# Two stacked GRU layers and a mixture of experts on one core: a PSUM bank for each gate, and PE work by gate

## What is computed

```python
def _gru_layer(x, Wih, Whh, bih, bhh):
    xg = jnp.einsum('bti,gi->tbg', x, Wih) + bih
    def step(h, xt):
        hg = h @ Whh.T + bhh
        xr, xz, xn = jnp.split(xt, 3, axis=-1)
        hr, hz, hn = jnp.split(hg, 3, axis=-1)
        r = jax.nn.sigmoid(xr + hr)
        z = jax.nn.sigmoid(xz + hz)
        n = jnp.tanh(xn + r * hn)
        h_new = (1.0 - z) * n + z * h
        return (h_new, h_new)
...
mixed = jnp.tanh(jnp.einsum('bte,he->bth', x, W_in) + b_in + ctx)
h1 = _gru_layer(mixed, Wih0, Whh0, bih0, bhh0)
h2 = _gru_layer(h1, Wih1, Whh1, bih1, bhh1)
gated = gate[:, None, :] * h2 + h2
x = x + jnp.einsum('bth,eh->bte', gated, W_out) + b_out
...
shared = jax.nn.silu(xf @ w1) * (xf @ w3) @ w2
h = jax.nn.gelu(jnp.einsum('nc,ech->enh', xf, W1e), approximate=False)
y = jnp.einsum('enh,ehc->enc', h, W2e)
routed = jnp.einsum('ne,enc->nc', combine, y)
x = x + (shared + routed) / 3
```

## Time and profile before

| | us |
|---|---|
| median of 3 runs | 2193.89 |
| lowest, highest | 2191.0, 2194.55 |
| span of the profiled execution | 2185.8 |
| PE busy | 2068.4 (95%) |
| PE's weight loads busy | 1485.0 (68%) |
| DVE busy | 1841.5 (84%) |
| ACT busy | 1201.4 (55%) |
| POOL busy | 560.5 (26%) |

### The profile page before, as it was taken

The page is one execution under the profiler, slowest core; times in us unless marked ns, Lnnn a source line. Parts: engine busy times, 40 slices in busy tenths (PEclk is TensorE's granted clock), DMA queues, the critical chain, the costliest instruction groups (busy, mean ns, idle before and its releaser), DMA issues.

```text
span 2185.8 us, 162058 instructions
## 1 busy us (share of the span) xinstructions
PE 2068.4 (95%) x69920; PEld 1485.0 (68%) x69920; DVE 1841.5 (84%) x11225; ACT 1201.4 (55%) x6471; POOL 560.5 (26%) x2542
## 2 busy tenths in 40 slices
PE   6989899999999999999999999999999999999987
PEld 3666666677666776767767676666767676777766
DVE  4888889888888888888888888888888888888874
ACT  2555555555555555555555555555555555555542
POOL 1222232222322223222222222222232222222220
PEclk9999999999999999999999999999999999999999
DMA  5000000000000000000000000000000000000000
GB/s 219 4 4 5 4 5 5 24 5 5 9 5 24 5 5 10 5 24 5 10 5 24 5 5 9 5 24 5 5 10 5 24 5 10 5 21 9 5 16 19
DMA packets 10879, 32.76 MB, mean 15 GB/s; under 512 B 1368, under 2 KB 6832, under 8 KB 9136
## 3 DMA queue, kind: packets, MB, share of 16 engines
q1 hardware_dynamic: 10160, 22.38, 2.8%
HBM read 20.22 MB, written 2.16 MB: 10 GB/s over the span
## 4 chain that ended last, share of the span: by engine, by line
PE 60%; DVE 26%; ACT 10%; issue 3%; DMA 1%; SPq 0%; POOL 0%; DVEq 0%; POOLq 0%
PE bank L333 29%; PE bank L325 17%; PE bank L272 11%; DVE n_first L404 9%; DVE cells L424 7%; ACT factors L472 6%; ACT cells L476 4%; DVE r_pre L395 4%; DVE z_pre L405 3%; PE bank L306 3%; DVE bank L413 1%; DVE n_second L380 0%; DVE x L687 0%; PE bank L657 0%; DVE hid L745 0%
## 5 line engine op out<-in xcount | busy, mean ns | idle before, releaser
L333 PE MATMUL bank<-w_h,cells 128*22 128x128 f32 (+4 forms) x32768 | 1363.4, 281 | 23.6 <-DVE cells L424 13.9
L333 PEld LDWEIGHTS bank<-w_h,cells 128*22 128x22 f32 (+4 forms) x32768 | 853.0, 111 | 130.5 <-DVE cells L424 91.3
L325 PEld LDWEIGHTS bank<-w_h,cells 128*2 128x2 f32 (+15 forms) x28112 | 512.2, 113 | 528.1 <-DVE cells L424 502.8
L517 POOL TENSOR_SCALAR cells<-cells 128x4 f32<-128x4 f32 x2048 | 463.6, 226 | 1525.8 <-DVE cells L424 1524.8
L325 PE MATMUL bank<-w_h,cells 128*2 128x64 f32 (+15 forms) x28112 | 770.1, 225 | 76.3 <-DVE cells L424 55.5
L466 ACT ACTIVATE n_second<-r_pre 128x4 f32<-128x4 f32 x2048 | 426.3, 208 | 508.8 <-DVE r_pre L395 466.3
L472 ACT ACTIVATE factors<-z_pre 128x4 f32<-128x4 f32 x2048 | 429.6, 210 | 436.5 <-DVE z_pre L405 358.8
L404 DVE STREAM_TRANSPOSE n_first<-bank 128x64 f32<-128x64 f32 x2048 | 600.0, 293 | 33.1 <-PE bank L333 23.7
L424 DVE TENSOR_TENSOR_SCAN cells<-factors,cells 128x18 f32<-128x18 f32 x2048 | 397.2, 194 | 241.5 <-ACT cells L476 177.1
L395 DVE STREAM_TRANSPOSE r_pre<-bank 128x64 f32<-128x64 f32 x2048 | 480.6, 235 | 33.3 <-PE bank L325 24.9
L405 DVE STREAM_TRANSPOSE z_pre<-bank 128x64 f32<-128x64 f32 x2048 | 427.4, 209 | 0.0
(11 more groups left out here) (91 smaller groups left out, 558.8 us busy)
## 6 DMA issues: line engine op xcount, KB each, us to landing
c_all<-weights SPq DMA_DIRECT2D x6, 1024.0 KB
x_t<-in_x_t SPq DMA_DIRECT2D x4, 512.0 KB, 7.4
w_1e<-in_w_1e SPq DMA_DIRECT2D x1, 2048.0 KB
w_2e<-in_w_2e SPq DMA_DIRECT2D x1, 2048.0 KB
w_x<-in_w_x SPq DMA_DIRECT2D x2, 768.0 KB, 8.2
w_h<-in_w_h SPq DMA_DIRECT2D x2, 768.0 KB, 9.5
w<-in_w SPq DMA_DIRECT2D x3, 512.0 KB
out_y<-y SPq DMA_DIRECT2D x6, 256.0 KB, 3.5
```

The lines of the kernel that those rows point to most:

```text
L325: mm = pe.matmul(r_sums[l][p][32 * g:32 * g + B * (j + 1)], state_tile(l, j, kt), w_h[l][:, kt, g, 2 * U:], start=False, stop=False, tile_ ...
L333: mm = pe.matmul(sums[l][p][32 * g:32 * g + B * (j + 1), 0:width], state_tile(l, j, kt), w_h[l][:, kt, g, 0:width], start=False, stop=Fals ...
L517: pool.tensor_scalar(cell_part(step_rows(l, j), 3), cell_part(step_rows(l, j), 1), 0.5, None, ALU.mult)\
```

## The change

There is now one bank for the r sums (0), one for the n sums (1) and one for the z sums (2), each used by both layers in both chunk halves. Bank 3 holds `sums` of both layers, which takes biases and projections alone. `r_first` and the form with 192 columns are gone: each step is 8 matmuls of 64 columns for r, 8 for n and 8 for z.

Since both layers now share banks, PE has new waits: before the n sums of a layer it waits until DVE has transposed the z sums of the other layer's step before it. DVE waits for each gate by itself. Once in a chunk and layer DVE fills three gates by copies where it filled one. Layer 1's r transpose stands ahead of layer 0's new state.

```diff
-        r_sums = [[banks[l][:, p * U:(p + 1) * U] for p in range(2)] for l in range(2)]
-        sums = [[banks[2 + l][:, p * NGATE * U:(p + 1) * NGATE * U] for p in range(2)] for l in range(2)]
+        r_sums, n_sums, z_sums = ([[bank[:, (2 * l + p) * U:(2 * l + p + 1) * U] for p in range(2)] for l in range(2)] for bank in banks[0:3])
+        sums = [banks[3][:, l * NGATE * U:(l + 1) * NGATE * U] for l in range(2)]
...
+        def gate_sums(pe, at, l, j, first):
+
+            for kt in range(KT):
+                for g in range(NQ):
+                    mm = pe.matmul(at[32 * g:32 * g + B * (j + 1)], state_tile(l, j, kt), w_h[l][:, kt, g, first:first + U],
+                                   start=False, stop=False, tile_position=(0, 32 * g), skip_group_check=True)
             return mm
...
-            if r_first(l, t):
-                for kt in range(KT):
-                    for g in range(NQ):
-                        mm = pe.matmul(r_sums[l][p][32 * g:32 * g + B * (j + 1)], state_tile(l, j, kt), w_h[l][:, kt, g, 2 * U:],
-                                       start=False, stop=False, tile_position=(0, 32 * g), skip_group_check=True)
-                mm.then_inc(s["r"], 1)
-            if j == 3 and places_biases(t):
-                pe.wait_ge(s["bias"], 1)
-            width = 2 * U if r_first(l, t) else 3 * U
-            for kt in range(KT):
-                for g in range(NQ):
-                    mm = pe.matmul(sums[l][p][32 * g:32 * g + B * (j + 1), 0:width], state_tile(l, j, kt), w_h[l][:, kt, g, 0:width],
-                                   start=False, stop=False, tile_position=(0, 32 * g), skip_group_check=True)
-            mm.then_inc(s["pe"], 1)
+            at = t + LAG * l
+            other, slot = (at - 1 - LAG, at - 1) if l == 0 else (at, at)
+            if l == 1 and t == 0:
+                pe.wait_ge(sets[0][other // CH % 2]["turn"], 2 * (other % CH) + 1)
+            gate_sums(pe, r_sums[l][p], l, j, 2 * U).then_inc(s["r"], 1)
+            if 0 <= other < T:
+                pe.wait_ge(sets[1 - l][other // CH % 2]["turn"], 2 * (other % CH) + 2)
+            gate_sums(pe, n_sums[l][p], l, j, 0).then_inc(s["n_pe"], 1)
+            if fills_next(1 - l, slot):
+                pe.wait_ge(sets[1 - l][slot // CH % 2]["xn"], 1)
+            gate_sums(pe, z_sums[l][p], l, j, U).then_inc(s["pe"], 1)
...
-                if t >= CH:
+                if t >= 0:
                     pe.wait_ge(sets[l][p]["bias"], 1)
-            if t >= 0:
-                pe.wait_ge(sets[l][p]["turn"], 2 * (t % CH) + 2)
-            mm = project_all(pe, l, 1 - p, kt)
+            mm = project_all(pe, l, kt)
...
+        def fill_r(v, l, p):
+
+            v.tensor_copy(r_sums[l][p], sums[l][:, 2 * U:3 * U])
+
+        def fill_n(v, l, p):
+
+            v.tensor_copy(n_sums[l][p], sums[l][:, 0:U])
+
+        def fill_z(v, l, p):
+
+            v.tensor_copy(z_sums[l][p], sums[l][:, U:2 * U]).then_inc(sets[l][1 - p]["xn"], 1)
...
                 if t0 is not None:
+                    dve_turn_n(v, 0, t0)
+                if fills[0]:
+                    fill_n(v, 0, q)
+                if t0 is not None:
+                    dve_turn_z(v, 0, t0)
+                if fills[0]:
+                    fill_z(v, 0, q)
...
-            if j == 2 and places_biases(t):
-                act.activation(sums[l][1 - p], biases[l][:], ACT.Identity).then_inc(s["bias"], 1)
+            if places_biases(l, t):
+                act.activation(sums[l], biases[l][:], ACT.Identity).then_inc(s["bias"], 1)
```

More of the change, by code:

```diff
@@ L96, in busy @@
         if engine == "act":
-            return ((j - LAG) if part else j) % CH == 2 or self.sparse and part == 1
-        return (j, part) in ((13, 0), (1, 1), (2, 1))
+            return (j, part) in ((3, 0), ((4 + LAG) % CH, 1)) or self.sparse and part == 1
+        return (j, part) in ((13, 0), (1, 1))
     def half(self, name):
@@ L386, in dve_turn_r, with dve_turn_n, dve_turn_z @@
             s = sets[l][p]
-            if r_first(l, t):
-                v.wait_ge(s["r"], sum(r_first(l, i) for i in range(t - j, t + 1)))
-                at = r_sums[l][p]
-            else:
-                v.wait_ge(s["pe"], j + 1)
-                at = sums[l][p][:, 2 * U:3 * U]
+            v.wait_ge(s["r"], j + 1)
             if j == CH - 1 and t < T - 1:
                 v.wait_ge(s["go"], 1)
-            v.transpose(r_pre[l][:].rearrange("p i b -> p b i"), blocks(at)).then_inc(s["turn"], 1)
-        def dve_turn_nz(v, l, t):
+            v.transpose(r_pre[l][:].rearrange("p i b -> p b i"), blocks(r_sums[l][p])).then_inc(s["turn"], 1)
+        def dve_turn_n(v, l, t):
+            p, j = t // CH % 2, t % CH
+            s = sets[l][p]
+            v.wait_ge(s["n_pe"], j + 1)
+            v.transpose(n_first[l][:, :, :, 2].rearrange("p i b -> p b i"), blocks(n_sums[l][p])).then_inc(s["for_n"], 1)
+        def dve_turn_z(v, l, t):
             p, j = t // CH % 2, t % CH
@@ L401, in dve_turn_nz @@
             v.wait_ge(s["pe"], j + 1)
-            if j == 0:
-                v.wait_ge(sets[l][1 - p]["xn"], 1)
-            v.transpose(n_first[l][:, :, :, 2].rearrange("p i b -> p b i"), blocks(sums[l][p][:, 0:U])).then_inc(s["for_n"], 1)
-            v.transpose(z_pre[l][:].rearrange("p i b -> p b i"), blocks(sums[l][p][:, U:2 * U])).then_inc(s["turn"], 1)
+            v.transpose(z_pre[l][:].rearrange("p i b -> p b i"), blocks(z_sums[l][p])).then_inc(s["turn"], 1)
         def dve_n(v, l, t):
@@ L411, in dve_n @@
             own = own_rows(j)
+            if j == 0:
+                v.wait_ge(sets[l][1 - p]["xn"], 2)
             v.wait_ge(s["for_n"], 2 * (j + 1))
@@ L428, in dve_slots @@
             for s, t0, t1 in schedule(s0, n):
[L429 to L431 removed]
+                q = 1 - s // CH % 2
+                fills = [fills_next(l, s) for l in range(2)]
+                if t0 is not None:
                     dve_turn_r(v, 0, t0)
+                if fills[0]:
+                    v.wait_ge(sets[0][1 - q]["x"], 1)
+                    fill_r(v, 0, q)
                 if 0 <= s - 1 - LAG < T:
                     dve_h(v, 1, s - 1 - LAG)
[L435 to L436 removed]
                 if t0 is not None:
[L438 removed]
+                    dve_turn_n(v, 0, t0)
+                if fills[0]:
+                    fill_n(v, 0, q)
+                if t0 is not None:
+                    dve_turn_z(v, 0, t0)
+                if fills[0]:
+                    fill_z(v, 0, q)
+                if t0 is not None:
                     dve_n(v, 0, t0)
[L440 to L443 removed]
+                if fills[0]:
+                    take_n(v, 0, q)
                 mixture_at(v, "dve", s, 0, base)
+                if t1 is not None:
+                    dve_turn_r(v, 1, t1)
+                if fills[1]:
+                    v.wait_ge(sets[1][1 - q]["x"], 1)
+                    fill_r(v, 1, q)
+                if fills[1] and t1 is None:
+                    fill_n(v, 1, q)
+                    fill_z(v, 1, q)
                 if t0 is not None:
@@ L447, in dve_slots @@
                 if t1 is not None:
-                    dve_turn_r(v, 1, t1)
-                    dve_turn_nz(v, 1, t1)
-                    dve_n(v, 1, t1)
-                if CH <= s < T + CH and j == 1:
-                    v.wait_ge(sets[1][p]["x"], 1)
-                    take_r(v, 1, 1 - p)
-                if CH <= s < T + CH and j == 2:
-                    take_n(v, 1, 1 - p)
+                    dve_turn_n(v, 1, t1)
+                    if fills[1]:
+                        fill_n(v, 1, q)
+                    dve_turn_z(v, 1, t1)
+                    if fills[1]:
+                        fill_z(v, 1, q)
+                    dve_n(v, 1, t1)
+                if fills[1]:
+                    take_n(v, 1, q)
                 mixture_at(v, "dve", s, 1, base)
@@ L893, in _ @@
             for kt in range(KT):
-                mm = project_all(pe, 0, 0, kt)
+                mm = project_all(pe, 0, kt)
             mm.then_inc(s_x0, 1)
```

62 lines of the change are left out of this document (26 added, 36 removed).

## The result

The changed kernel takes 3155.41 us (median of 4 runs, 3152.33 to 3159.97), the kernel before 2193.92: a ratio of 1.4385 [1.4364, 1.4405]. The prediction was 3,066 us, with blocks of instructions as the limit.

What follows compares the result with a forecast made beforehand. PE's instruction blocks, brought one at a time, were taken as the limit: 815 blocks at 3.6 us make 2,934 us, plus 130 at start and end, less 6, a span of 3,058; with 8 for launch 3,066 us, range 2,400 to 3,260.

Steps and rivals of the forecast that it cites:

- The bound now: Kernel before: PE uses an instruction block in 3.87 us, just slower than a round of 3.4 to 4.0 us.
- Streaming time: PE's gate sums: the same 192 columns per weight tile in a step, so they stream as long as before; cost none.
- first rival: Blocks come early enough and PE's new wait before n limits: 2,238 us, between 2,180 and 2,290; chance 0.13.
- The count: PE's instructions: 292 blocks more, 841 where there were 548, of which 815 in the slots with both layers.
- The round: Time per PE instruction block: 3.6 us, mean of three stalls, bounds 3.2 and 4.0; 815 blocks make 2,934 us.
- The wait at n: PE before n sums, for the other layer's z transpose: 2.0 us a loop, costing nothing inside a 2.9 us slot.
- The transposes: DVE transposes n while PE makes z: a step alone loses 0.17 us, 6 us gained over 38 steps.
- The fills: DVE's three copies where there was one: at most 0.15 us in 128 slots, 19 us, hidden if blocks limit.
- The start: Start of the kernel: some 100 more PE instructions, counted towards the blocks without a time of their own.
- The launch above the span: Whole execution: the launch lies 8 us above the span, 2,193.89 against 2,185.8, added to the sum.
- The clock: PE's granted clock: stalls of about 1 us per block should leave it at 1.00; otherwise the time grows further.
- The Trainium skill: Its page holds PE's instruction fetch to be hidden; by it the block term would be zero; the prediction disagreed.

Runs made afterwards that it cites:

- b_half: The kernel before, in r-first steps with half as many gate matmuls of twice the columns, second half of the state left out: 2139.00 us, 0.973.
- a_half: The changed kernel with half as many gate matmuls, each of twice the columns, second half of the state left out: 2242.98 us, 1.0203.
- a_waits: The changed kernel in full, with n waiting for the other layer's transpose of n and z for that of z: 3104.89 us, 1.4221.
- b_split: The kernel before with only its n and z sums split into 64-column matmuls, banks and waits unchanged: 3163.30 us, 1.439.
- b_light: The kernel before with four of 16 steps in the 192-column form from the start on: 2180.97 us, 0.9933.
- b_two: The kernel before with PE's other work as two matmuls of 64 rows instead of four of 32: 2272.94 us, 1.0413.
- b_wide: The kernel before with PE's other work as one matmul of 128 rows instead of four of 32: 2302.69 us, 1.0461.
- b_best: The kernel before with other work as one 128-row matmul, layer 1's r transposed early and r first in every step: 2381.63 us, 1.0821.
- a_wide: The changed kernel with PE's other work as one matmul of 128 rows instead of four of 32: 3039.07 us, 1.3825.
- b_first: The kernel before with r made first in every step, none in the 192-column form: 2222.88 us, 1.018.

## Why the prediction was right, point by point

**The bound now.** The reading of the earlier trace rows, that PE used a block in 3.87 us and could get one in 3.4 to 4.0, was right, and more so than it said: the kernel before was losing 24 to 59 us to blocks (b_half), where the row it named had 13.6.

**Streaming time, no cost.** It can't be told apart under the blocks in full size. In a_half, with as many columns, the measured time is within 5 us of the first rival's sum, which had no term for streaming. Some of that nearness is luck: the slots with both layers took 2,113 us (1,005 of 2.10) where the sum had 2,106, and the launch above the span 2 us where it had 8.

**The count.** 841 blocks were predicted, the page has 840. For the stretch with both layers 815 were taken, the window holds 812.

**The round.** This is the term that was mis-sized: 3,026.5 us over 812 blocks is 3.73 us where the mean of three stalls gave 3.6. That is 3,026.5 against 2,934, 92 of the 100 us by which the span of 3,158.2 exceeds the predicted 3,058. The other 8 lie outside that stretch, 131.7 us where the sum had 124 (see the start). A slot is therefore 3.01 us and not 2.7 to 2.9, and PE is 75% busy, not some 70%. The round stands within the bounds of 3.2 and 4.0 that made the range; single ones, as the 4.02 above, don't. Of the 92 us, 27 are rounding: the mean of 3.5, 3.4 and 4.0 is 3.63, and 815 x 3.63 is 2,961. Three stalls were too few to fix a mean to 3%, and in two of them PE had stood 2.4 to 2.7 us with nothing to run, which hardly any round of the changed kernel does (5 stalls in all are over 2.3 us).

**The wait at n.** "It costs nothing there" was wrong by 1.1% (a_waits), some 35 us: over a third of the round's excess. Its price without blocks was right: 2,238 predicted for that rival, 2242.98 measured in a_half.

**The transposes.** 1.77 us was predicted for a step alone, 1.79 is measured (median of the first 19). That gain exists only in the 38 slots with one layer.

**The fills** at 19 us under the blocks: nothing speaks against it, and no run measured it apart.

**The start.** "Some 100 instructions" more were given no cost. They cost 7 us: the first new state comes at 26.34 us where it came at 19.53. PE rows of the changed kernel:

```profile
14.63 0.59 PE L293 MATMUL bank<-hist,ones 128*32 128x256 f32 x2
15.06 0.67 PE L297 MATMUL bank<-hist,ones 128*32 128x64 f32 x9
```

The bias matmuls, 64 in the trace, took 2.4 us before (14.26 to 16.69); now they are 112 and take 7.6 (14.63 to 22.25). The new code writes 7 matmuls in a row on one strip of 32 partitions, then 7 on the next; before it was 2 and 2. Now they take 68 ns each where it was 38: they overlap less. That it is this order no run tested.

**The launch above the span.** 8 us was taken from the median and the profiled span. In the changed kernel the profiled execution took 3159.97 us with a span of 3158.2: 1.8 us. So the 8 us of before were probably for the most part the distance between the profiled execution and the median one, and this term was 6 us too high, in the other direction.

**The clock.** It stayed at 1.00 but for moments (0.996 in the mean), as the 0.89 us stall of the earlier trace rows suggested. The stalls are 1.03 us in the mean.

**The Trainium skill.** "Runtime: NRT & Kernel Launch", section "Instruction fetch mechanics", has the blocks of 256 right, 840 by count and 256 instructions between two stalls. Its other statement, that the fetch is mostly hidden, would have given the first rival's 2,238 us; the measured 3155.41 and b_split's 3163.30 decide against it for an engine that needs 256 instructions in under 3.7 us.

## What to carry to other kernels

Count an engine's instructions as you count its columns: on PE, 256 of them took about 3.7 us in the mean here when the engine was never out of work, so a slot has a budget, and splitting a matmul to free a bank or to start a reader earlier spends it. A kernel near that budget shows little "issue" time (27.5 us in 2,186 here) and can still be slowed, so try an edit that changes the count alone, as b_split or b_light, before one that changes the order. And where a wait protects a bank, let it wait for the last reader of that bank and no more: here that was worth 6% once the blocks were out of the way.

## What the runs showed of the hardware

- PE's instruction blocks come one after the other: 840 blocks, 822 stalls, 3.73 us a round in the mean; a transfer begins 2.42 us before PE goes on, the next 1.15 us after (medians of 755 stalls). In the kernel before, the page's 1.7% of 16 engines' span for 548 blocks are 1.1 us for the transfer of one, so most of a round is not the transfer.
- A weight load of 64 or 128 columns behind loads for strips of 32 leaves PE idle for 0.2 us, 742 and 730 times (b_two, b_wide); one of 32 columns doesn't. Behind the 128-column piece the loads for strips wait again, 0.33 us in b_best.
- What a block is worth depends on how far the kernel is over the limit: 3.6 us where every round is full (a_wide, 118 us for 33), some 1.8 at its edge (b_first) and 1.2 below it (b_light). The last two are estimates, with the 192-column form's 0.18 us a slot taken out; as measured, net of it, they are 1.1 and 0.5.
